# Post-norm layer with ternary weights and a top-k gate: setup rebuilt, output weights loaded late, z kept unscaled, some flags in other PSUM banks, and the last activation on VectorE

## The reference

```python
x1  = layernorm(x + x @ (W + delta_W).T)                  # 512 x 512
z   = x1 @ ternary(W_syn).T + b_syn                       # 2048 values a token
thr = 204th largest of each token's z
h   = where(z >= thr, relu(z), 0)
out = h @ ternary(W_out).T + b_out                        # back to 512
y   = layernorm(layernorm(x1 + out) * gamma + beta)
```

## Time and profile before

| | |
|---|---|
| profiled execution | 658.22 us |
| its span in the profile | 656.4 us |
| median of 3 runs | 658.97 us |
| TensorE, VectorE, ScalarE, GpSimd busy | 581.0, 545.0, 554.5, 378.8 us (89, 83, 84, 58%) |
| first `below` starts | 73.36 us |
| fourth and 29th `below` start | 131.62 and 568.05 us |
| last `below` starts | 619.54 us |

### The profile page before, as it was taken

How to read it: one execution, slowest core, us unless ns; L and a number is a source line. 1 busy time by engine, 2 the same in 40 slices (tenths; PEclk the granted TensorE clock), 3 DMA queues, 4 the chain that set the end, 5 groups by cost and what they waited for, 6 DMA issues and landing times. The chain is left out here.

```text
span 656.4 us, 8334 instructions
## 1 busy us (share of the span) xinstructions
PE 581.0 (89%) x2374; PEld 254.5 (39%) x2374; DVE 545.0 (83%) x649; ACT 554.5 (84%) x729; POOL 378.8 (58%) x712
## 2 busy tenths in 40 slices
PE   0769478999999999999999999999999999897552
PEld 0324133444444444444444444444444444342221
DVE  4557787899899898999989989989989999988761
ACT  2866766899999999999999999999999999988732
POOL 0023585566666666666666666666666666666632
PEclk9779797999999999999999999999999999998777
DMA  8952044254546454645455454535564444443340
GB/s 341 391 147 49 16 96 81 55 104 83 114 96 129 98 128 97 128 82 127 97 105 120 75 116 88 115 80 124 97 130 96 98 96 88 89 97 80 81 92 36
DMA packets 184481, 71.62 MB, mean 109 GB/s; under 512 B 168048, under 2 KB 176240, under 8 KB 183792
## 3 DMA queue, kind: packets, MB, share of 16 engines
q1 hardware_dynamic: 184432, 71.07, 48.4%
HBM read 20.72 MB, written 8.39 MB: 44 GB/s over the span
## 5 line engine op out<-in xcount | busy, mean ns | idle before, releaser
L507 ACT ACTIVATE junk<-z_sb,t_col 128x2048 f16<-128x2048 f32 x128 | 254.9, 1992 | 11.9 <-POOL t_col L406 10.9
L886 PE MATMUL z_ps<-t_syn,xhT 128*128 128x512 f16 x1024 | 234.1, 383 | 6.4 <-DMA xhT<-xh 5.8
L886 PEld LDWEIGHTS z_ps<-t_syn,xhT 128*128 128x128 f16 x1024 | 100.8, 99 | 139.5 <-issue 27.4
L896 PE MATMUL o_ps<-t_out,hT 128*128 128x512 f16 x512 | 122.8, 396 | 19.0 <-DMA hT<-hh 17.0
L871 PE MATMUL u_ps<-weff,xT_sb 128*128 128x512 f32 x256 | 120.1, 614 | 21.6 <-DVE weff L639 16.7
L387 POOL TENSOR_SCALAR tmp<-signs,dev 128x1 f32<-128x1 f32 x64 | 47.3, 739 | 140.2 <-ACT junk L507 140.1
L902 PE MATMUL o_ps<-t_out,hT 128*128 128x512 f16 x512 | 120.1, 389 | 0.0
L779 DVE SCALAR_TENSOR_TENSOR z_sb<-z_sb,thr 128x2048 f32<-128x2048 f32 x32 | 75.3, 2352 | 31.2 <-DVE flag L758 18.2
L745 DVE SCALAR_TENSOR_TENSOR z_sb<-z_ps,sc,bias_z 128x1024 f32<-128x1024 f32 x64 | 81.9, 1279 | 9.5 <-PE z_ps L886 9.5
L543 ACT ACTIVATE hh<-z_sb 128x2048 f16<-128x2048 f32 x32 | 61.1, 1911 | 30.7 <-DVE z_sb L779 30.7
L718 DVE SCALAR_TENSOR_TENSOR w_sb<-z_sb,t_col 128x2048 f32<-128x2048 f32 x32 | 75.2, 2352 | 13.2 <-POOL t_col L406 13.2
(11 more groups left out here) (116 smaller groups left out, 562.4 us busy)
## 6 DMA issues: line engine op xcount, KB each, us to landing
xT_sb<-in_xT SPq DMA_DIRECT2D x16, 512.0 KB, 4.7
out_y<-y_sb SPq DMA_DIRECT2D x32, 256.0 KB, 2.9
z_sb<-in_w_synT SPq DMA_DIRECT2D x4, 1024.0 KB, 13.1
hh<-in_w_outT SPq DMA_DIRECT2D x2, 1024.0 KB, 18.8
...
```

What stands on the lines that cost most here:

```text
L507: a_.activation(junk[:, n % 2, :], z_sb[:, t % ZS, :], ACT.Sign, bias=at, scale=-1.0, accum_out=signs[:, j, r:r + 1]).then_inc(counted, 1)
L886: last = mm(z_ps[:, c, b * BANK:(b + 1) * BANK], xhT[:, j, h * KD + k, :], t_syn[:, k, n0:n0 + BANK], start=k == 0 and h == 0, stop=k == K ...
L896: mm(o_ps[t % OS][:, :], hT[:, j, 0, c, :], t_out[:, c, :], start=c == 0, stop=False)
```

## The change

- `ln3_out` moves from ScalarE (after `hi_x`) to VectorE, one step later, between `general(f)` and `hidden(f)`.
- z is kept unscaled: `evac` scales by the mean alone, `hi_h` takes the power of two as a scale pointer, `lo_h` becomes a scalar_tensor_tensor with the same pointer; the scaling of the bias row is gone, and `SPREAD` is 1.2945.
- The flags of tiles 0 to 2 go to `o_ps`, those of tiles 28 to 31 to `u_ps`. For these tiles `mm2(s, 1)` stands right behind `mm2(s, 0)` and doesn't wait for the flag.
- W and delta_W are loaded and combined in halves, matmuls wait for each slice; TensorE runs 30 + 3 x 8 matmuls of `ones` before and between the first products. The sums of |W_syn| are shared by ScalarE and VectorE; W_out's loads are issued behind the first transpose; the first steps' orders are new on all engines.
- At the end `add_beta` comes before `mean_r`, and `count(31, 4)` before `square2`.

```diff
+EARLY, BETWEEN = 30, 8
...
+        def flag_at(t):
+            if t < OS:
+                return o_ps[t][0:1, 0:1]
+            return u_ps[0:1, 0:1] if t >= TILES - TAIL else z_ps[0:1, 1, 0:1]
...
+            def load_out(k):
+                dst = out_in[k].rearrange("p (c d) -> p c d", d=D)
+                sp.dma_start(dst, outw_v[:, QB * k:QB * (k + 1), :]).then_inc(out_loaded[k], 16)
+            wT_v, dwT_v = (a.rearrange("(k p) n -> p k n", p=P) for a in (wT, dwT))
+            for h in range(2):
+                sp.dma_start(weff[:, 2 * h:2 * h + 2, :], wT_v[:, 2 * h:2 * h + 2, :]).then_inc(weff_loaded[h], 16)
+                sp.dma_start(dw_in[:, 2 * h:2 * h + 2, :], dwT_v[:, 2 * h:2 * h + 2, :]).then_inc(weff_loaded[h], 16)
             load(0)
+            sp.dma_start(b_in[:, :], b_syn.rearrange("(p a) -> p a", p=P)).then_inc(b_loaded, 16)
...
             transpose_x(0)
+            sp.dma_start(bias_z[:, :], b_syn.rearrange("(a n) -> a n", a=1).broadcast_to([P, N]))\
+                .then_inc(bsyn_loaded, 16)
+            load(1)
+            load_out(0)
+            load_out(1)
+            load_out(2)
+            transpose_x(1)
+            load_out(3)
+            for k, src in enumerate((b_out, gamma, beta)):
+                sp.dma_start(vecs[:, k, :], src.rearrange("(a n) -> a n", a=1).broadcast_to([P, D])).then_inc(vec_loaded, 16)
             load(2)
-            for s in range(LAST + 2):
+            for s in range(1, LAST + 2):
...
             bias_norm()
-            scales(-2)
             sigma()
             scales(-1)
             for s in range(LAST + 1):
                 l, e = s - L_MM3, s - L_OUT
+                if s > TILES and live(l):
+                    add_beta(l)
                 if live(l):
                     mean_r(l)
                 if live(s):
...
                 wait(act, hiT[t % 2], 16 * (t // 2))
-                a_.activation(hh[:, t % 2, 0, :], z_sb[:, t % ZS, :], ACT.Copy).then_inc(h_hi, 1)
+                a_.activation(hh[:, t % 2, 0, :], z_sb[:, t % ZS, :], ACT.Copy, scale=sc[:, 6:7]).then_inc(h_hi, 1)
...
             square1(-3, 0)
+            ln1_out(-3, 0)
+            hi_x(0)
+            sum_syn(2, 0, N)
+            sum_syn(3, 1, HALF)
+            square1(-2, 1)
             sign_syn(0)
             sign_syn(1)
-            ln1_out(-3, 0)
-            hi_x(0)
-            for i in range(2, 6):
-                sign_syn(i)
-            square1(-2, 1)
-            sign_syn(6)
-            sum_nnz()
+            sign_syn(2)
             ln1_out(-2, 1)
             hi_x(1)
-            sign_syn(7)
+            sign_syn(3)
+            sign_syn(4)
+            sum_nnz()
+            for i in range(5, 8):
+                sign_syn(i)
             sum_out(0)
+            square1(-1, 2)
             sum_out(1)
-            square1(-1, 2)
-            sum_out(2)
             count(0, 0)
             first_step(0)
             ln1_out(-1, 2)
...
                     first_step(s)
                 if live(a):
                     square1(s, a)
+                if s == TILES:
+                    count(s - 1, 4)
                 if live(l):
                     square2(s, l)
-                if live(s - 1):
+                if live(s - 1) and 1 < s < TILES:
                     count(s - 1, 4)
                 if live(s):
                     count(s, 1)
                     second_step(s)
+                if s == 1:
+                    count(0, 4)
+                if live(s):
                     count(s, 2)
                 if live(a):
                     ln1_out(s, a)
                     count(s, 3)
                 if live(a):
                     hi_x(a)
-                if live(e):
-                    ln3_out(s, e)
                 if live(l):
                     square3(s + 1, l)
...
+            def first_weights(h):
+                ks = range(2 * h, 2 * h + 2)
+                dve.wait_ge(weff_loaded[h], 32)
+                for k in ks:
+                    v.scalar_tensor_tensor(weff[:, k, :], weff[:, k, :], 1.0, dw_in[:, k, :], ALU.mult, ALU.add,
+                                           accum_out=wsum[:, k:k + 1]).then_inc(setup_step, 1)
+                nstep[0] += 2
+                dve.wait_ge(setup_step, nstep[0])
                 dve.wait_ge(consts_made, 1)
...
+                nstep[0] += 2
+                link(v.tensor_scalar(wmean[:, 2 * h:2 * h + 2], wsum[:, 2 * h:2 * h + 2], 1.0, -U_SCALE / D, ALU.add, ALU.mult))
+                for k in ks:
+                    v.tensor_scalar(weff[:, k, :], weff[:, k, :], U_SCALE, wmean[:, k:k + 1], ALU.mult, ALU.add)\
+                        .then_inc(weff_made, 1)
+            def sum_syn(k, n0, i):
+                dve.wait_ge(syn_loaded[k], 16)
+                src = syn_in[k][:, n0:N]
+                link(v.scalar_tensor_tensor(w_sb[:, n0:N], src, -1.0, src, ALU.mult, ALU.max, accum_out=psyn[:, i:i + 1]))
...
-                v.tensor_tensor(hh[:, j, 1, :], z_sb[:, t % ZS, :], hh[:, j, 0, :], ALU.subtract).then_inc(h_lo, 1)
+                v.scalar_tensor_tensor(hh[:, j, 1, :], z_sb[:, t % ZS, :], sc[:, 6:7], hh[:, j, 0, :], ALU.mult,
+                                       ALU.subtract).then_inc(h_lo, 1)
...
+            def ln3_out(s, t):
+                dve.wait_ge(b3_ready, t + 1)
+                wait(dve, stored[t % 2], 16 * (t // 2))
+                v.tensor_scalar(y_sb[:, t % 2, :], o_ps[t % OS][:, :], rs[:, s % 2, 2:3], b3[:, s % 2:s % 2 + 1],
+                                ALU.mult, ALU.add).then_inc(y_ready, 1)
+            first_weights(0)
+            first_weights(1)
             first_sums()
+            sum_syn(0, 0, 0)
+            lo_x(0)
+            sum_syn(1, 0, 1)
+            sum_syn(3, HALF, KD)
+            syn_scale()
             for i in range(3):
                 syn_weights(i)
-            lo_x(0)
-            for i in range(3, 8):
+            spread()
+            syn_weights(3)
+            lo_x(1)
+            for i in range(4, 7):
                 syn_weights(i)
+            spread_out()
+            evac(0, 0)
+            syn_weights(7)
+            evac(0, 1)
             scaling()
-            lo_x(1)
-            spread()
-            evac(0, 0)
-            evac(0, 1)
+            sum_out(2)
+            evac(1, 0)
             sum_out(3)
-            scale_vecs()
-            evac(1, 0)
             out_part()
             lo_x(2)
+            evac(1, 1)
             out_scale()
             out_weights(0)
-            evac(1, 1)
-            out_weights(1)
-            evac(2, 0)
             below(0)
             top8(0)
+            out_weights(1)
             select(0)
             lo_x(3)
+            evac(2, 0)
             general(0)
             hidden(0)
+            scale_vecs()
+            evac(2, 1)
             out_weights(2)
-            evac(2, 1)
             lo_h(0)
             out_weights(3)
...
-            for s in range(3, LAST + 1):
-                f, l, d, a = s - L_SEL, s - L_MM3, s - L_LN2, s + A_X
+            for s in range(3, LAST + 2):
+                f, l, d, e, a = s - L_SEL, s - L_MM3, s - L_LN2, s - 1 - L_OUT, s + A_X
+                if s == 3:
+                    evac(s, 0)
...
                     centre(s, d)
                 if live(f):
                     general(f)
+                if live(e):
+                    ln3_out(s - 1, e)
+                if live(f):
                     hidden(f)
                 if live(d):
                     add_v(s, d)
-                if live(s):
+                if live(s) and s > 3:
                     evac(s, 0)
                 if live(f):
...
+                if c == 1 and OS <= t - L_SEL < TILES - TAIL:
+                    pe.wait_ge(flag_read, t - L_SEL + 1)
                 wait(pe, z_evac, 2 * t + c - 1)
                 for k in range(KD):
+                    if t == 0:
+                        pe.wait_ge(t_syn_made, c * KD + k + 1)
...
+                if t < OS:
+                    pe.wait_ge(flag_read, t + 1)
...
+            def flags(t):
                 pe.wait_ge(selected, t + 1)
-                pe.wait_ge(z_evac, 2 * upto(s - 1))
                 wait(pe, flag_read, t)
-                mm(z_ps[0:1, 1, 0:1], ones[:, 0:1], ok[:, t % 2:t % 2 + 1], start=True, stop=True).then_inc(flag_ready, 1)
+                if t >= TILES - TAIL:
+                    pe.wait_ge(x1_ready, TILES)
+                elif t >= OS:
+                    pe.wait_ge(z_evac, 2 * upto(t + 1))
+                mm(flag_at(t), ones[:, 0:1], ok[:, t % 2:t % 2 + 1], start=True, stop=True).then_inc(flag_ready, 1)
...
+            def keep_busy(n):
+                for _ in range(n):
+                    mm(z_ps[:, 1, BANK:BANK + P], ones[:, :], ones[:, :], start=True, stop=True)
             pe.wait_ge(consts_made, 1)
-            pe.wait_ge(weff_made, KD)
+            keep_busy(EARLY)
             mm1(0)
+            keep_busy(BETWEEN)
+            mm1(1)
```

(60 more changed lines are left out.)

52 lines of the change are left out of this document (10 added, 42 removed).

## The result

The kernel after the change takes 667.8 us (median of 4 runs, 667.0 to 669.0), the one before, on the same chip, 659.0. The ratio is 1.0136, with a 95% interval of 1.0119 to 1.0154: slower by 1.4%. The forecast was 661.3, slower, in a range of 645 to 668. The profiled execution has a span of 666.1 against 656.4.

A forecast was written before the change was run, and what follows sets the result against it. TensorE was taken to bound the turns, with the selection's ring 0.2 to 0.3 us behind. Span 656.4 - 10.3 (setup) + 11.1 (25 turns) + 2.1 (three turns) - 0.6 (end) = 658.7; median 661.3 us, range 645 to 668.

The forecast's parts named there:

- the ring: Cross-engine chain from one `below` to the next; 17.2 us a turn without TensorE, 17.9 with the change, above TensorE's 17.46.
- ScalarE's 0.76: In the turns: the 0.76 us a turn ScalarE loses gives nothing, since it waits for `hidden` and GpSimd anyway.
- The forecast's own case: Whole kernel: setup gains, the turns lose more; 661.3 us, own range 656 to 666, chance 0.55.
- rival 3: Setup: the busy matmuls take 0.5 us each and delay the start; 666 us, chance 0.11.
- Rival 1: Turns: TensorE stays the bound at 17.46 us, the selection's chain absorbing `ln3_out`'s 0.66; 647 us, chance 0.22.
- rival 2: Setup gives more, 14 to 17 us, through warm TensorE and earlier flags; 656 us, chance 0.09.
- rival 4: Exact loop: changed roundings send a tile through 25 `max` passes and replacements; +115, 775 us, chance 0.03 with the like.
- Setup (a) to (f): Start to `below(3)`: six steps from the weight loads through the first turns, together 10.3 us earlier, given 7 to 14.
- step (c): Setup: x1's transpose queues behind nothing but W_syn, so the second `evac` starts at about 41.5, 9.3 us earlier.
- Step (f): Setup: with `mm2(s, 1)` ahead of the flag, two turns take 16.2 and 17.5 us; `below(3)` at 121.3.
- The turns: Tiles 3 to 28: `ln3_out` adds 0.66 and `hi_h`'s pointer 0.04 a turn; +11.1 us over 25 turns.
- The end: Tile 31: `ok` 0.67 us earlier through `top8`, another 0.5 by preceding `add_beta`, `ln3_out(28)` returning 0.66; -0.6 us net.

The follow-up runs named there:

- y_alone: The kernel before with only `ln3_out` moved, to VectorE between `general` and `hidden`: 675.8 us, ratio 1.0252.
- y_on_scalar: The changed kernel with `ln3_out` back on ScalarE, in its old place behind `hi_x`: 649.3 us, ratio to before 0.9844.
- early_loads: y_on_scalar with x's second pair and all four parts of W_out loaded ahead of the first transpose of x1: 658.3 us, ratio 0.9992.
- cold: y_on_scalar without the 54 matmuls of ones: 651.0 us, ratio 0.9876.
- flags_in_z: y_on_scalar with all flags in `z_ps` and `mm2(s, 1)` behind `mm3_lo` in every step, as before: 649.7 us, ratio 0.986.
- warm_pick: flags_in_z plus 28 matmuls of ones ahead of the matmuls of tiles 30 and 31, and `add_beta` beside `ok(31)` waiting until it ends: 645.9 us.

## Why the prediction was right, and where its sizes were off

The mechanism was the forecast's: `ln3_out` stands in the ring, ScalarE's 0.76 gives nothing, and the ring passes TensorE. The size was not, and that the time lies in the range is in part luck. The forecast's own case was to end between 656 and 666, and 667.8 lies outside it; it is 0.2 under the upper end of 668, which was put there to take in rival 3. The kernel got 8.8 us slower by the medians where 2.3 were forecast, and the 25 turns cost 17.0 where +3 to +15.5 was given. All terms behind the setup came out too low, and the setup gained 1.2 more than forecast, which hid a part of that.

Rival 1 (the ring absorbs it) is refuted by y_alone, and its 647 is near what y_on_scalar has (649.3), where the ring doesn't get the instruction. Rival 3 fails by the matmul of ones at 9.54 / 30 = 0.32 us, near my 0.37; rival 2 by the start of `below(3)`, 11.5 earlier and not 14 to 17; rival 4 by the groups, in which no pass of `match_replace` stands.

*Setup (a) to (f).* `mm1(0)` ended at 15.1 (15.5 forecast), the thresholds' chain was done at 24.4 (25), the second `evac` started at 39.8 (41.5), `below` of tiles 0, 1, 3 at 59.4, 86.7, 120.2 (60.4, 87.6, 121.3). The forecast's -10.3 was -11.5; y_on_scalar, with the same setup, has -10.5, so about 1 of it differs between profiled executions, with the time at which x lands. early_loads confirms step (c), the transpose behind the loads, as the largest part; the ones bring about 1.3 (cold). Step (f) had the length of the two turns (33.4 measured, 33.7 forecast) but not the reason: by flags_in_z they are as short without the early `mm2(s, 1)`. What shortened them against before isn't shown.

*The turns: the term that was mis-sized.* I had 17.9 where 18.14 was measured, and 25 times 0.24 is the 6 us that are missing in the sum. The parts, each small and all of one sign: `ln3_out` 0.73 to the next start and not 0.66 (it takes 0.81, more than the 0.75 of the row I took it from); the idle time behind the branch 0.94 and not 0.87; `hi_h` with a pointer 0.09 and not 0.04; `lo_h`, which was put "beside the ring" at no price, adds 0.06 to it, over GpSimd's L408; together 0.25. The lesson is the multiplier: with 25 turns, 0.05 in one link is 1.3 us, the whole resolution of the measurement. The same excess over the three turns behind them explains +3.1 for +2.1.

The group of `ln3_out` over the turns (line, shapes, count; busy, mean ns; idle before by releaser) is the row that was lacking before:

```profile
L839 DVE TENSOR_SCALAR y_sb<-o_ps,rs,b 128x512 f32<-128x512 f32 x25 | 20.3, 810 | 24.6 <-DVE flag L791 20.7 <-issue 3.9
```

0.81 out of PSUM, against 0.48 for the first and 0.42 start to start from SBUF. The rule of the Trainium skill that the prediction named ("VectorE: DVE Perf Modes", section "Why PSUM operands drop a tier") agrees with it. For the pointer a sentence of the Trainium skill would have given the right end ("ScalarE: Activation LUTs", section "What ACT_TABLE_LOAD costs": a pointer operand adds about 93 ns to an ACTIVATE); the two traces agree, 2.00 and 1.91.

*The end: the step that failed in sign.* I expected `ok(31)` 0.67 earlier and 0.5 ahead of `add_beta`. The timeline of VectorE in after:

```profile
633.12 1.31 DVE L765 SCALAR_TENSOR_TENSOR ok<-m,t_col,hit 128x1 f32<-128x1 f32 x1
...
659.25 0.75 DVE L826 SCALAR_TENSOR_TENSOR o_ps<-o_ps,rs,x1g 128x512 f32<-128x512 f32 x1
```

`ok(31)` did start earlier, 4.98 after `below(31)` instead of 5.61, but met the addition and took 1.31 instead of 0.69: it ended 6.29 after `below(31)`, as before (6.30). Then `ln3_out` and the longer idle time (0.80) came on top, 0.07 from `hidden(31)` to `mm3_hi(31)`, where the pointer of `hi_h` is, and 0.35 for `mm3_hi(31)` itself, which took 5.30 at a granted clock of 0.68 and 4.95 at 0.72 before. `add_beta` ahead of the mean gave 0.15 back behind the last matmul (0.1 was forecast). The last `add_v` is 31.11 behind `below(31)` where it was 30.03: the whole +1.1. warm_pick shows that the theory of the 0.5 was right and only the order was not: with the addition behind `ok`, the 1.1 are won.
